# Leaving out the semaphore waits that an engine's earlier wait already covers, in a two-layer transformer kernel on 8 cores

## The chip, the cores and the metric

The kernel runs on the 8 cores of one Trainium2 chip. Every core runs the same program on its own rows. The metric is the device time in microseconds of the slowest core. Five engines of a core take part: TensorE (PE), VectorE (DVE), ScalarE (ACT), GpSimd (POOL) and SyncE (SP). Each works through its own list of instructions in order, and they meet only at semaphores.

## The reference, cut to what matters

Four sub-layers follow each other, each with a residual and a layer norm around it:

```python
x = _layernorm(x + _L0_attn_ref(x, ...))   # 16 heads, one shared K and V of width 64, softmax over 4096 keys
x = _layernorm(x + _L0_ffn_ref(x, ...))    # 4096-wide FFN, top-1 LoRA expert of 8
x = _layernorm(x + _L1_attn_ref(x, ...))   # third-order attention on a window of the last 32 keys
x = _layernorm(x + _L1_ffn_ref(x, ...))    # 8 SwiGLU experts, top-4 weights
```

The input is 4 x 4096 x 1024 in float32.

## The kernel before

Two cores share one of the 4 sequences. A core owns 2048 rows (16 tiles of 128, in the SBUF buffer `resid`) and also reads the other half for the keys and values of the first attention. The work is written as phases, one after the other:

- **kv** (`phA_kv_all`): for 32 row tiles in turn a layer norm (`ln_tile`: DVE, two tiny ACT functions at L126 and L128, DVE again), 8 transposes on PE (L523), a copy on ACT (L531), the K product (L544) and the V product (L552), and two copies on ACT (L561, L564). The ACT functions of the next tile stand behind these copies in ACT's list.
- **four rounds of q, attention, wo** (`phA_q`, `phA_attn`, `phA_wo`), each for 512 rows. Attention goes over 16 heads, and for each head over 16 key blocks kp of 256 keys. `emit_qk` (L731) makes two 512-column products into one of two PSUM slots, `emit_exp` (L742) is one exponential of 128x1024 on ACT into one of three SBUF slots, and `emit_pv` (L753) makes two products with V. PE's list has QK(kp+1) before PV(kp). The end of head h is written out after kp = 1 of head h+1 (`epilogue`): a reciprocal of 1x512 on DVE (L766), a broadcast product on PE (L770), a copy on ACT (L776) and a product on DVE (L780). It stands ahead of QK(3) in PE's list.
- **B** (`phaseB`): the first FFN, 32 groups of 9 products (L989, L995) with a ReLU on ACT (L1004) and then the second matrix (L1036), for four groups of 512 rows; the routing work (`emit_prep`, `rank_counts`) stands in between.
- **C** (`phaseC`): the windowed attention of the last 128 rows, head by head, and 16 tiles of layer norms.
- **D** (`phaseD`): routing of 16 tiles (L1337, L1357), then 8 experts x 2 halves: 32 pairs of gate and up products (L1457, L1464), each with two ACT and three DVE instructions (L1476 to L1498), and then the down product (L1517) of 8 tiles. **Out** writes the result.

`run_phase` calls a phase's function once for each engine, each time with a new object of the class `Em`. `Em` counts every semaphore (TT, VV, SS, GG are bumped by PE, DVE, ACT and POOL; the lanes LX, LW and SO by DMAs) and puts out only the instructions of its own engine. A wait is asked for by `E.w(engine, semaphore, value)` or, for a DMA, by `E.wt(engine, token)`; `E.dma` asks for one on its lane itself. Before the change each of these calls puts one wait instruction of its own into the engine's list, ahead of the instruction that it guards. So an instruction can have several waits ahead of it. The one for the exponential, in `emit_exp`:

```python
        E.w("s", "TT", qkv)           # QK(kp) is done
        E.w("s", "TT", lps[pslot])    # the PV that last read this slot is done
```

Semaphores only count up, and both waits are on TT. PE's list has PV(kp-3) before QK(kp), so the value of the second is never above that of the first.

Of the kernel before, what the change touches and what calls it, by code (L numbers as in the profile page):

```python
# [34 lines left out]
class Ctr:  # L35
    __slots__ = ("sem", "n", "step")

    def __init__(self, sem, step=1):
        self.sem, self.n, self.step = sem, 0, step
# [7 lines left out]
class Em:  # L47
    def __init__(self, k, eng, C):
        self.k, self.e, self.C = k, eng, C

    def dma(self, pool, key, f):
        idx = self.C["_pool_" + pool]
        names = LANES[pool]
        name = names[idx.n % len(names)]
        idx.n += 1
        c = self.C[name]
        self.w(key, name, c.n)
        c.n += 16
        tok = (name, c.n)
        if self.k == key:  # L60
            f(self.e).then_inc(c.sem, 16)
        return tok

    def wt(self, key, tok):
        if tok and self.k == key:
            self.e.wait_ge(self.C[tok[0]].sem, tok[1])

    def op(self, key, f, inc=None):
# [10 lines left out]

    def w(self, key, cname, val):  # L80
        if self.k == key and val and val > 0:
            self.e.wait_ge(self.C[cname].sem, val)

    def t(self, f, inc=None):
# [1482 lines left out]
def host_prep(inputs):  # L1567
# [7 lines left out]
    def ktile(w):  # L1575
        K, N = w.shape
        return np.ascontiguousarray(
            w.reshape(K // 128, 128, N).transpose(1, 0, 2).reshape(128, -1))
# [74 lines left out]
```

## Time and profile before

| | us |
|---|---|
| median of the two timed runs | 7444.8 |
| the two runs | 7669.35 and 7220.25 |
| the profiled execution, its device time | 7291.01 |
| its span, slowest core (core 3) | 7289.2 |
| spans of the eight cores | 7185.3 to 7289.2 |
| granted TensorE clock, mean over the cores of die 0 / die 1 (medians) | 0.862 / 0.872 |

A busy share is a mean over phases with different limits. The page's slices and the table by stretch show where PE is full and where the engines take turns. "Idle before" is the time for which an engine had nothing running ahead of an instruction, with what ended it. Wait instructions themselves are not shown as busy: their time is part of these idle times.

### The profile page before, as it was taken

How to read it: one execution, taken by the hardware profiler on the slowest of the kernel's cores; microseconds unless marked ns; L12 is line 12 of the kernel's file. 1: busy time of each engine (PE TensorE's matmuls, PEld its weight loads, DVE VectorE, ACT ScalarE, POOL GpSimd, SP SyncE). 2: the span in 40 equal slices, each digit the busy share in tenths (PEclk: the TensorE clock that was granted, in tenths of full speed). 3: DMA queues.
4: the chain of work that ended last, by engine and by line, in shares of the span. 5: the costliest groups of instructions: out<-in, count | busy, mean ns of one | idle time of the engine just before them, and what ended most of it. 6: DMA issues, size and time to landing. Idle time of an engine off the chain costs nothing.

```text
span 7289.2 us, 67922 instructions; the slowest of 8 cores (7185.3 to 7289.2 us)
## 1 busy us (share of the span) xinstructions
PE 5151.0 (71%) x22235; PEld 2083.4 (29%) x22235; DVE 2548.8 (35%) x5344; ACT 2241.3 (31%) x3440; POOL 246.8 (3%) x428
## 2 busy tenths in 40 slices
PE   2367577577576675673110498989989898989996
PEld 1222222222222222221000243434434343434332
DVE  6521311312213101102447543444434444444334
ACT  1257377376584110111220222222222222222211
POOL 0000000000000000000000000000000000000000
PEclk9989799799798887786555599999999999999787
DMA  2100000100100555565000223232332324232321
GB/s 65 41 12 1 12 12 1 23 1 1 24 1 14 104 93 93 105 115 92 0 0 0 41 49 64 47 66 45 56 58 47 70 47 70 47 70 47 63 36 58
DMA packets 61633, 326.06 MB, mean 45 GB/s; under 512 B 7218, under 2 KB 7490, under 8 KB 46544
## 3 DMA queue, kind: packets, MB, share of 16 engines
q0 software_dynamic: 54400, 296.50, 23.1%
q1 hardware_dynamic: 6896, 25.23, 1.0%
q8 instruction: 193, 3.16, 0.2%
q14 instruction: 144, 1.18, 0.1%
HBM read 609.63 MB, written 8.39 MB: 85 GB/s over the span
## 4 chain that ended last, share of the span: by engine, by line
PE 56%; DVE 16%; ACT 12%; DMA 7%; issue 6%; POOL 1%; DVEq 0%; ACTq 0%; POOLq 0%; SPq 0%
PE pB L1517 13%; PE pA L1457 12%; ACT pTs L742 7%; PE pA L1464 6%; PE pB L1464 6%; PE pA L753 4%; DMA wobuf<-woT 3%; DVE rrec L766 3%; PE pB L731 3%; PE pB L1036 3%; DMA wgu<-guT 2%; PE pA L989 2%; DMA wibuf<-wiT 1%; DVE lnt L143 1%; PE pB L614 1%
## 5 line engine op out<-in xcount | busy, mean ns | idle before, releaser
L742 ACT ACTIVATE pTs<-pB,cbias 128x1024 bf16<-128x1024 f32 x1024 | 1095.6, 1110 | 280.7 <-PE pB L731 275.5
L1457 PE MATMUL pA<-x3T,wgu 128*128 128x512 bf16 x4096 | 1005.8, 390 | 122.8 <-DMA wgu<-guT 104.4
L1476 ACT ACTIVATE r7D<-pA,g7mb 128x512 f32<-128x512 f32 x512 | 351.8, 687 | 2278.7 <-PE pA L1464 1696.9
L1517 PE MATMUL pB<-dnTsb,actT 128*128 128x512 bf16 x4096 | 971.7, 399 | 72.1 <-DVE actT L1498 72.1
L753 PE MATMUL pA<-pTs,vones 128*128 128x512 bf16 x2048 | 611.2, 379 | 287.2 <-ACT pTs L742 284.0
L1486 DVE SCALAR_TENSOR_TENSOR t1D<-r7D,sgD 128x512 f32<-128x512 f32 x512 | 354.4, 692 | 805.2 <-ACT sgD L1481 805.2
L766 DVE RECIPROCAL rrec<-pA 1x512 f32<-1x512 f32 x64 | 214.7, 3355 | 1128.6 <-PE pA L753 1094.9
L731 PE MATMUL pB<-qhT,kT 128*128 128x512 bf16 x2048 | 604.1, 382 | 0.5 <-ACT cbias L714 0.5
L1517 PEld LDWEIGHTS pB<-dnTsb,actT 128*128 128x128 bf16 x4096 | 405.6, 102 | 630.5 <-issue 271.7
L1457 PEld LDWEIGHTS pA<-x3T,wgu 128*128 128x128 bf16 x4096 | 381.4, 99 | 681.2 <-issue 355.1
L1464 PE MATMUL pA<-x3T,wgu 128*128 128x512 bf16 x2048 | 500.8, 389 | 0.0
L1464 PE MATMUL pB<-x3T,wgu 128*128 128x512 bf16 x2048 | 496.1, 386 | 0.0
L1532 DVE SCALAR_TENSOR_TENSOR resid<-pB,ncomb,resid 128x1024 f32<-128x1024 f32 x128 | 164.3, 1284 | 884.3 <-PE pB L1525 884.3
L1036 PE MATMUL pB<-wobuf,interT 128*128 128x512 bf16 x1024 | 285.8, 447 | 163.9 <-DMA wobuf<-woT 151.5
L1498 DVE SCALAR_TENSOR_TENSOR actT<-r7D,t1D 128x512 bf16<-128x512 f32 x512 | 354.4, 692 | 54.5 <-DVE r7D L1491 1.4
L753 PEld LDWEIGHTS pA<-pTs,vones 128*128 128x128 bf16 x2048 | 136.4, 96 | 743.6 <-issue 729.3
L1481 ACT ACTIVATE sgD<-r7D 128x512 f32<-128x512 f32 x512 | 322.3, 630 | 47.9 <-ACT r7D L1476 1.5
L126 ACT ACTIVATE stat<-stat 128x1 f32<-128x1 f32 x144 | 29.6, 206 | 911.2 <-DVE stat L124 911.1
L1059 DVE TENSOR_TENSOR ytmpB<-pB,resid 128x1024 f32<-128x1024 f32 x16 | 19.5, 1221 | 740.5 <-PE pB L1050 740.5
L1464 PEld LDWEIGHTS pA<-x3T,wgu 128*128 128x128 bf16 x2048 | 205.0, 100 | 256.9 <-issue 49.9
L989 PE MATMUL pA<-x1T,wibuf 128*128 128x512 bf16 x1024 | 252.2, 391 | 32.7 <-ACT interT L1004 18.1
L1464 PEld LDWEIGHTS pB<-x3T,wgu 128*128 128x128 bf16 x2048 | 203.2, 99 | 250.8 <-issue 39.4
(235 smaller groups left out, 3759.4 us busy)
## 6 DMA issues: line engine op xcount, KB each, us to landing
wgu<-guT POOLq DMA_DIRECT2D x256, 512.0 KB, 5.1
wobuf<-woT POOLq DMA_DIRECT2D x64, 1024.0 KB, 10.0
wibuf<-wiT POOLq DMA_DIRECT2D x32, 1024.0 KB, 8.9
dnTsb<-dnT POOLq DMA_DIRECT2D x8, 4096.0 KB, 25.9
w<-w POOLq DMA_DIRECT2D x5, 2048.0 KB, 16.5
resid<-xb SPq DMA_DIRECT2D x4, 2048.0 KB
wbuf<-wq POOLq DMA_DIRECT2D x4, 2048.0 KB, 16.2
xst<-xb SPq DMA_DIRECT2D x16, 512.0 KB
```

Of the source, the lines that this page charges most:

```text
L731: r = E.t(lambda e, kc=kc, sub=sub, slot=slot, qoff=qoff: e.matmul(pB[slot][:, sub * 512:(sub + 1) * 512], A["kT"][:, kc * 128:(kc + 1) * ...
L742: les[slot] = E.s(lambda e, slot=slot, pslot=pslot: e.activation(out=A["pTs"][:, pslot * 1024:(pslot + 1) * 1024], in_=pB[slot][:, 0:1024] ...
L753: r = E.t(lambda e, kc=kc, sub=sub, pslot=pslot, pva=pva: e.matmul(pva[:, 0:512], A["vones"][:, kc * 128:kc * 128 + 128], A["pTs"][:, pslo ...
L766: vr = E.v(lambda e, pva=pva: e.reciprocal(A["rrec"][64:65, 0:512], pva[64:65, 0:512]), "VV")
L989: E.t(lambda e, c8=c8, p=p, gid=gid, pg=pg: e.matmul(pg[:, 0:512], Bd["wibuf"][:, (gid % 2) * 4096 + c8 * 512 + (p % 4) * 128: (gid % 2) * ...
L1036: r = E.t(lambda e, p=p, pp=pp, tl=tl, tli=tli, half=half, wid=wid: e.matmul(pB[tli][:, half * 512:(half + 1) * 512], Bd["interT"][:, p * ...
L1457: E.t(lambda e, c8=c8, gid=gid, pg_ap=pg_ap, xoff=xoff: e.matmul(pg_ap, Dd["wgu"][gid % 2][:, c8 * 128:(c8 + 1) * 128], Dd["x3T"][:, c8 * ...
L1464: r = E.t(lambda e, c8=c8, gid=gid, pu_ap=pu_ap, xoff=xoff: e.matmul(pu_ap, Dd["wgu"][gid % 2][:, 1024 + c8 * 128:1024 + (c8 + 1) * 128], ...
L1476: sr7 = E.s(lambda e, so=so, pg_ap=pg_ap, j=j: e.activation(out=Dd["r7"][:, so:so + 512], in_=pg_ap, func=AF.Relu, scale=-1.0, bias=Dd["g7 ...
L1486: vt1 = E.v(lambda e, so=so: e.scalar_tensor_tensor(out=Dd["t1"][:, so:so + 512], in0=Dd["r7"][:, so:so + 512], scalar=7.0, in1=Dd["sg"][: ...
L1498: act_vv[par] = E.v(lambda e, so=so, aoff=aoff: e.scalar_tensor_tensor(out=Dd["actT"][:, aoff:aoff + 512], in0=Dd["r7"][:, so:so + 512], s ...
L1517: E.t(lambda e, kc=kc, half=half, t8=t8, pw=pw: e.matmul(pw[:, half * 512:(half + 1) * 512], Dd["actT"][:, kc * 1024 + (t8 // 4) * 512 + ( ...
```

## The change

`Em` gets a table of the highest value that its engine has waited for on each semaphore in this phase. A wait whose value is not above that is not put out. Nothing else is changed: no instruction that computes, no DMA, no order, no buffer. As the table is new with each `Em`, it starts empty in each phase.

```diff
 class Em:
     def __init__(self, k, eng, C):
         self.k, self.e, self.C = k, eng, C
+        self.hwm = {}
@@
     def wt(self, key, tok):
         if tok and self.k == key:
+            if tok[1] <= self.hwm.get(tok[0], 0):
+                return
+            self.hwm[tok[0]] = tok[1]
             self.e.wait_ge(self.C[tok[0]].sem, tok[1])
@@
     def w(self, key, cname, val):
         if self.k == key and val and val > 0:
+            if val <= self.hwm.get(cname, 0):
+                return
+            self.hwm[cname] = val
             self.e.wait_ge(self.C[cname].sem, val)
```

## Rows read from the trace of the kernel before

**Rows 1.** The page: busy time by engine, and the chain by engine

```profile
PE 5151.0 (71%) x22235; PEld 2083.4 (29%) x22235; DVE 2548.8 (35%) x5344; ACT 2241.3 (31%) x3440; POOL 246.8 (3%) x428
...
PE 56%; DVE 16%; ACT 12%; DMA 7%; issue 6%; POOL 1%; DVEq 0%; ACTq 0%; POOLq 0%; SPq 0%
```

**Rows 2.** Busy time by stretch (PE, PEld, DVE, ACT, POOL; PEclk): attention, two experts

```profile
932.00:1286.00 354.00, 275.20 (x1050) 84.62 (x1050) 61.20 (x31) 281.87 (x273) 0.00 (x0) 1.00 0.04 7
...
5315.00:5694.00 379.00, 352.65 (x1572) 148.93 (x1573) 158.58 (x212) 84.71 (x129) 17.96 (x34) 0.96 0.32 56
...
6834.00:7208.00 374.00, 364.96 (x1373) 146.69 (x1372) 140.54 (x187) 75.11 (x115) 14.25 (x27) 0.81 0.23 38
```

**Rows 3.** Timeline of attention: start, duration, engine, line; in brackets idle before

```profile
1500.94 2.12 ACT L742 ACTIVATE pTs<-pB,cbias 128x1024 bf16<-128x1024 f32 x2 [0.32 <-PE pB L731]
...
1502.17 0.13 PEld L753 LDWEIGHTS pA<-pTs,vones 128*128 128x128 bf16 x2 [0.87 <-issue]
1502.20 0.59 PE L753 MATMUL pA<-pTs,vones 128*128 128x512 bf16 x2 [0.41 <-ACT pTs L742]
...
1502.63 0.59 PE L731 MATMUL pB<-qhT,kT 128*128 128x512 bf16 x2
...
1503.38 2.12 ACT L742 ACTIVATE pTs<-pB,cbias 128x1024 bf16<-128x1024 f32 x2 [0.32 <-PE pB L731]
```

**Rows 4.** Timeline of attention from one head to the next

```profile
523.61 2.12 ACT L742 ACTIVATE pTs<-pB,cbias 128x1024 bf16<-128x1024 f32 x2 [0.92 <-PE pB L731]
...
540.51 3.35 DVE L766 RECIPROCAL rrec<-pA 1x512 f32<-1x512 f32 x1 [16.74 <-PE pA L753]
...
544.09 0.19 PEld L770 LDWEIGHTS pA<-rrec,ones 1*64 1x64 f32 x2 [0.81 <-issue]
544.12 1.04 PE L770 MATMUL pA<-rrec,ones 1*64 1x512 f32 x2 [0.34 <-DVE rrec L766]
...
545.85 1.11 ACT L742 ACTIVATE pTs<-pB,cbias 128x1024 bf16<-128x1024 f32 x1 [0.92 <-PE pB L731]
```

**Rows 5.** Timeline of kv: one row tile, and the same product of the next

```profile
201.09 0.61 PE L552 MATMUL pA<-wkv_sb,xnT 128*128 128x64 bf16 x8
...
201.78 0.21 ACT L564 CAST vones<-pA 128x64 bf16<-128x64 f32 x1 [0.28 <-PE pA L552]
...
206.22 1.01 PE L523 MATMUL pF<-idb,xnb 128*128 128x128 bf16 x8 [4.53 <-DVE xnb L145]
...
207.38 1.01 ACT L531 COPY xnT<-pF 128x1024 bf16<-128x1024 bf16 x1 [4.99 <-PE pF L523]
...
208.61 0.82 PEld L544 LDWEIGHTS pA<-xnT,wkv_sb 128*64 128x64 bf16 x8 [1.65 <-issue]
...
214.75 1.01 PE L523 MATMUL pF<-idb,xnb 128*128 128x128 bf16 x8 [4.54 <-DVE xnb L145]
```

**Rows 6.** Timeline of C: a layer norm's first instruction behind two waits

```profile
3861.35 0.69 DVE L118 BATCH_NORM_STATS2 stat<-Pf 128x6 f32<-128x512 f32 x1 [0.17 <-DVE Pf L1311]
```

**Rows 7.** Timeline of D: a pair's end, the next pair, and the down product's start

```profile
5001.97 1.89 PE L1464 MATMUL pA<-x3T,wgu 128*128 128x512 bf16 x8
...
5003.70 1.89 PE L1457 MATMUL pA<-x3T,wgu 128*128 128x512 bf16 x8
...
5024.89 0.69 DVE L1498 SCALAR_TENSOR_TENSOR actT<-r7D,t1D 128x512 bf16<-128x512 f32 x1
5026.02 1.00 PEld L1517 LDWEIGHTS pB<-dnTsb,actT 128*128 128x128 bf16 x6 [4.94 <-issue]
```

**Rows 8.** Chain in order of time: ends of the weight wait before three experts

```profile
5276.40 21.75 DMA wgu<-guT
...
5655.28 20.90 DMA wgu<-guT
...
6800.73 17.08 DMA wgu<-guT
```

**Rows 9.** One line of D, its last down tile: first and last start

```profile
L1532 DVE SCALAR_TENSOR_TENSOR resid<-pB,ncomb,resid x128: 1283/1284/1286, 4281.1 to 7229.4; 128x1024 f32<-128x1024 f32 x128
```

## The prediction

> **What bounds the kernel now.** I read the page first: no engine is full over the span, PE is busy 71%, and the chain that ended last is PE for 56%, DVE for 16% and ACT for 12% [rows 1]. Then the busy time by stretch, which splits the kernel in two kinds [rows 2]. In an expert of D, PE is busy 352.65 of 379 us: one engine streams. In an attention round ACT is busy 281.87 and PE 275.20 of 354 us: neither is full, they take turns. In kv DVE, PE and ACT take turns too, as the timeline shows: PE has stood idle 4.53 us before L523, ACT 4.99 us before L531 [rows 5]. Removed waits can matter only where engines take turns, since there every step from one engine to the next stands in the time. Then I read the timeline at such handovers, and that is where the reader should look: at the time between the end of one engine's work and the start of the next one's.
>
> Attention [rows 3]: the two exponentials that start at 1500.94 are followed by the next two at 1503.38, 2.44 us later, of which ACT is busy 2.12. The first ends at 1500.94 + 1.11 = 1502.05. PV's weight load starts at 1502.17, PV at 1502.20, QK at 1502.63, it ends at 1503.22, and the next exponential starts at 1503.38. So exp(kp), PV(kp), QK(kp+2), exp(kp+2) is a closed loop, and it sets the pace, not ACT (2.12) and not PE (8 products of 0.215 us, 1.72).
>
> **The change part by part.** It only removes wait instructions. I counted them from the code, engine by engine and phase by phase: 3161 of 14108 waits go, 1788 on PE, 1159 on ACT, 169 on DVE, 37 on POOL and 8 on SP. Of PE's 1096 and ACT's 1081 are in the four attention rounds, and 394 of PE's are in D.
>
> *Price of one wait.* The trace gives handovers with one wait and with more.
> - ACT after PE. One wait: L552 ends at 201.09 + 0.61 = 201.70 and L564 starts at 201.78, 0.08. Two: L523 ends at 207.23 and L531 starts at 207.38, 0.15 [rows 5]. The exponential with its two waits: 0.16 [rows 3]. The rows are rounded to 0.01, so a second wait costs 0.05 to 0.07; I take 0.06.
> - PE after ACT. One wait: 1502.05 to 1502.17, 0.12 [rows 3]. Two: L531 ends at 208.39 and L544's load starts at 208.61, 0.22 [rows 5]. After DVE with two: 540.51 + 3.35 = 543.86 to 544.09, 0.23 [rows 4]. With four: 5024.89 + 0.69 = 5025.58 to 5026.02, 0.44 [rows 7]. So 0.10 to 0.11 for each further wait; I take 0.11.
> - DVE: L118 behind two waits starts 0.17 after the end of the instruction that it waits for [rows 6]. No row shown has the same instruction behind one wait; the bounds are nothing and the 0.11 of PE, and I take 0.07, nearest to ACT.
>
> The Trainium skill, Advanced Engine Details and Errata, section Miscellaneous Facts, puts reading a semaphore from the sequencer at 50 to 100 ns, and the two prices above agree with it. VectorE: DVE Perf Modes, section The DRAIN you can't avoid, says that a semaphore after each of 8 copies cost nothing extra on DVE. By that rule the DVE term below would be nothing in place of 2.2 us.
>
> *Where a wait is hidden.* A wait that was satisfied long ago costs nothing if PE still has products queued. In each step of attention one of the waits that go stands between PV and QK, yet QK starts 1502.63 - 1502.20 = 0.43 us after PV, two products of 0.215 [rows 3]. In D two or three waits stand before each new pair; the pair at 5003.70 starts 1.73 us after the eight products that started at 5001.97, 0.216 each [rows 7]. So the 1033 removed waits before QK and the 302 before pairs in D are worth nothing: running products cover them. If that cover were gone, each would cost 0.11. A removed wait also gains nothing if it stands ahead of the wait that really blocks.
>
> *The sum, from handovers that are on the chain and where a removed wait follows the blocking one.*
> - Attention. One head's chain runs exp 3, 5, ..., 15, then PV, the reciprocal, L770, QK(3), and exp 3 of the next head (523.61 to 545.85) [rows 4]. On it are 7 exponentials with a second wait, and L770 with one: 7 x 0.06 + 0.11 = 0.53 us. The exponentials in between are in the same kind of loop and get shorter by the same, so they don't take over. L770 sits waiting for the reciprocal (0.34 idle), so that leg stays the longer one. Of the 64 heads I count 60, since at each round's start the clock is low and PE is the limit. 60 x 0.53 = 31.8.
> - kv. The next tile's norm waits in ACT's list behind this tile's last copy, so each tile is one chain of 214.75 - 206.22 = 8.53 us [rows 5]. L523, L544 (PE) and L531 (ACT) each lose a second wait: 31 x (0.11 + 0.11 + 0.06) = 8.7.
> - q. 16 tiles of the same form, with two waits on PE (L614, L645) and two on ACT (L601, L625): 16 x 0.34 = 5.4.
> - D. Before L1517 three waits behind the blocking one, 15 times: 15 x 0.33 = 5.0. Routing, L1357, 15 x 0.11 = 1.7.
> - B. Before L1036 about 15 waits: 1.7. Its other removed waits stand first or are covered.
> - wo and C. L118 32 times on DVE at 0.07, 2.2; ACT's L1211 15 times at 0.06, 0.9. Together 3.1.
> - POOL and SP: 45 waits ahead of DMA issues that are made early. Nothing; if each was on the path at PE's price, 5.
>
> Sum 57.4 us. Against the profiled execution: 7291.0 - 57.4 = 7234 us. The two runs shown lie at 7220.25 and 7669.35, so their median of 7444.8 is a mean of two unlike numbers. The profiled execution lies near the faster, and the forecast is for an execution of its kind. From 7220.25 the same sum gives 7163.
>
> **The rivals.**
> - *Nothing is gained.* Something next to the shortened loop takes over, or the handover ends on the slower of two legs anyway. For it: DVE's reciprocal (3.35) and the exponentials (1.11) stay as they are. Against: ACT stands idle 0.32 of each 2.44 and PE has idle time too [rows 3], and in kv nothing that matters runs beside the chain. Time 7291.
> - *Every removed wait counts,* since the engine's instruction stream is the limit. Then 1788 x 0.11 + 1159 x 0.06 + 169 x 0.07 = 197 + 70 + 12 = 279, and the time is 7012, faster by 3.8%. Against it speaks the spacing of 0.215 across a wait in rows 3 and 7. It passes 2% (146 us) when 89 us beyond my sum, about 810 of PE's waits, prove exposed.
> - *Slower: a lower granted clock for longer.* From 6834 on the granted clock is 0.81 of the 2.4 GHz level, where the expert before it in rows 2 has 0.96. The full-clock expert runs from 5276.40 + 21.75 = 5298.15 to 5655.28, 357.1 us; the last one from 6817.81 to 7229.4, 411.6 us [rows 8, 9]. So an expert at 0.81 costs 54 us more. The change makes PE denser in attention (0.53 us of each head) and lets D begin earlier; if the lower clock came three experts sooner, the gain is gone twice over: 7234 + 163 = 7397. Slower by 2% (7437) needs 3.7 experts more; all of the other 6.8 give 7601, which is near the slower run shown. For it: such a run exists already. Against: that run was of the kernel before, and the whole attention round at full clock (1.00) [rows 2] with PE at 78% did not bring it on.
>
> **How the numbers follow.** The forecast has 0.78, nothing gained 0.06, every wait 0.06, the clock 0.10, of which 0.07 is beyond 2% and 0.03 within. About 2% is what a measurement of this kernel can tell from no change. So faster 0.06, same 0.78 + 0.06 + 0.03 = 0.87, slower 0.07. The forecast alone spans 7150 to 7270: from 7291 the prices at their low ends and only attention and kv counted give 7291 - (60 x 0.45 + 31 x 0.25) = 7256, and from 7220.25 with a third more waits exposed it is 7144. The range is 7140 to 7400: down to that, and up to three experts more at the lower clock.
>
> **What would show it.** In the profile after: the page's instruction count falls from 67922 by 3161. Pairs of exponentials start 2.38 us apart and not 2.44, and ACT's idle before L742 falls from 0.32 to 0.26. The kv tiles come 8.25 us apart and not 8.53. L770's load starts 0.12 after the reciprocal, L1517's 0.12 after L1498. A full-clock expert still takes 357 us. I am wrong if the pairs of exponentials keep their distance, if experts at the same clock get shorter or longer, or if the lower clock covers another part of D than before.

## The result, and the profile after

| | before | after |
|---|---|---|
| median of all timings, us | 7635.29 (10) | 7472.83 (11) |
| lowest timings, us | 7219.94, 7220.25, 7223.72, 7226.57 | 7157.43, 7157.84, 7158.30 |
| profiled execution, us | 7291.01 | 7157.53 |
| ratio after to before | | 0.991, 95% interval 0.9891 to 0.993 |

In the other timings of both kernels (7601 to 7729 before, 7304 to 7683 after) the granted clock of one die, in 7585.86 of both, is lower than in the lowest ones, whatever the kernel, so the ratio comes from the lowest ones alone. The change takes 0.9% off, clear of nothing but below 2%. That is 64 us, where the sum of the prediction was 57.4. The forecast of 7234 and its range of 7140 to 7400 missed the median of all timings, 7472.83; the three lowest timings lie inside the range.

The page of the changed kernel: instructions, busy time, granted clock in 40 slices, and the chain.

```profile
span 7156.0 us, 64761 instructions; the slowest of 8 cores (7119.6 to 7156.0 us)
...
PE 5065.1 (71%) x22235; PEld 2058.0 (29%) x22235; DVE 2548.6 (36%) x5344; ACT 2239.5 (31%) x3440; POOL 246.9 (3%) x428
...
PEclk9989799799898887786555599999999999999998
...
PE 56%; DVE 17%; ACT 12%; DMA 8%; issue 5%; POOL 1%; DVEq 0%; ACTq 0%; POOLq 0%; SPq 0%
```

The count has fallen from 67922 to 64761, by exactly the 3161 waits that were counted. DVE's and ACT's busy time is as in [rows 1]. PE's is 86 us less, but the count of products is the same: core 3 of the profile before ran part of D at the lower clock [rows 2], and this one did not. So the difference of the two profiled spans, 133 us, is not the change's. I compare a core whose granted clock over D is 0.97 in both, which is called full clock below.

One attention pair in the timeline of the changed kernel (L749 is L742 before, L760 is L753, L738 is L731), to be held against [rows 3]:

```profile
1471.08 2.12 ACT L749 ACTIVATE pTs<-pB,cbias 128x1024 bf16<-128x1024 f32 x2 [0.26 <-PE pB L738]
...
1472.30 0.13 PEld L760 LDWEIGHTS pA<-pTs,vones 128*128 128x128 bf16 x2 [0.81 <-issue]
1472.33 0.59 PE L760 MATMUL pA<-pTs,vones 128*128 128x512 bf16 x2 [0.35 <-ACT pTs L749]
...
1472.76 0.59 PE L738 MATMUL pB<-qhT,kT 128*128 128x512 bf16 x2
...
1473.45 2.12 ACT L749 ACTIVATE pTs<-pB,cbias 128x1024 bf16<-128x1024 f32 x2 [0.26 <-PE pB L738]
```

The exponential ends at 1472.19 and PV's load starts at 1472.30, 0.11 later (before 0.12). QK ends at 1473.35 and the exponential starts at 1473.45, 0.10 later, where it was 0.16. All of the gain of this loop is in that one handover, and the pairs are 2.37 apart where they were 2.44.

The end of a head (L773 is L766, L777 is L770), against [rows 4], and a tile of kv (L530 is L523, L538 is L531, L551 is L544), against [rows 5]:

```profile
529.12 3.35 DVE L773 RECIPROCAL rrec<-pA 1x512 f32<-1x512 f32 x1 [16.08 <-PE pA L760]
...
532.59 0.19 PEld L777 LDWEIGHTS pA<-rrec,ones 1*64 1x64 f32 x2 [0.76 <-issue]
```

```profile
202.00 1.01 PE L530 MATMUL pF<-idb,xnb 128*128 128x128 bf16 x8 [4.42 <-DVE xnb L152]
...
203.10 1.01 ACT L538 COPY xnT<-pF 128x1024 bf16<-128x1024 bf16 x1 [4.83 <-PE pF L530]
...
204.23 0.82 PEld L551 LDWEIGHTS pA<-xnT,wkv_sb 128*64 128x64 bf16 x8 [1.48 <-issue]
...
210.26 1.01 PE L530 MATMUL pF<-idb,xnb 128*128 128x128 bf16 x8 [4.42 <-DVE xnb L152]
```

The load behind the reciprocal starts 532.59 - 532.47 = 0.12 after it (before 0.23). In kv the copy starts 0.09 after the transposes (before 0.15), the product's load 0.12 after the copy (before 0.22), and a tile takes 8.26 us (before 8.53).

The down product's start in D (L1524 is L1517, L1505 is L1498), against [rows 7], and the norm's first instruction in C (L125 is L118), against [rows 6]:

```profile
4973.52 0.69 DVE L1505 SCALAR_TENSOR_TENSOR actT<-r7D,t1D 128x512 bf16<-128x512 f32 x1
4974.32 0.13 PEld L1524 LDWEIGHTS pB<-dnTsb,actT 128*128 128x128 bf16 x2 [4.62 <-issue]
```

```profile
3791.09 1.22 DVE L1318 TENSOR_TENSOR Pf<-attC,resid 128x1024 f32<-128x1024 f32 x1
3792.41 0.69 DVE L125 BATCH_NORM_STATS2 stat<-Pf 128x6 f32<-128x512 f32 x1
```

The load starts 4974.32 - 4974.21 = 0.11 after its input, where it was 0.44 with three more waits. The norm starts 3792.41 - 3792.31 = 0.10 after its input, where it was 0.17 with one more wait. That is the price of 0.07 on DVE, which the prediction had to take between two bounds.

Where the kernel's stages end, on core 4 of both profiles, from the first and last start of the exponentials and of the down product's last step in the views by line. Before:

```profile
L742 ACT ACTIVATE pTs<-pB,cbias x1024: 1105/1113/1115, 430.2 to 2272.4; 128x1024 bf16<-128x1024 f32 x171
L1532 DVE SCALAR_TENSOR_TENSOR resid<-pB,ncomb,resid x128: 1283/1284/1286, 4284.7 to 7154.3; 128x1024 f32<-128x1024 f32 x128
```

After:

```profile
L749 ACT ACTIVATE pTs<-pB,cbias x1024: 1105/1113/1115, 421.9 to 2217.7; 128x1024 bf16<-128x1024 f32 x171
L1539 DVE SCALAR_TENSOR_TENSOR resid<-pB,ncomb,resid x128: 1283/1284/1286, 4230.7 to 7096.4; 128x1024 f32<-128x1024 f32 x128
```

| stretch, us | before | after | gain | sum of the prediction |
|---|---|---|---|---|
| start to the first exponential (kv, first q) | 430.2 | 421.9 | 8.3 | 8.7 + 1.4 |
| first to last exponential: four rounds | 1399.9 | 1366.9 | 33.1 | 31.8 |
| and the three gaps between them (wo, q) | 442.3 | 428.9 | 13.3 | 5.6 |
| to the first down product (last wo, B, C, routing) | 2012.3 | 2013.1 | -0.8 | about 5 |
| to the last down product (D) | 2869.6 | 2865.7 | 3.9 | 5.0 |
| end | 59.8 | 59.6 | 0.3 | 0 |

The fourth line is not still. On the eight cores of one profile it takes 1999 to 2019 us before and 1997 to 2013 after, and 1993 to 2015 in the experiments that leave B and C as before. One execution of the changed kernel with two waits more in attention (below) has it at 1983 to 2000, and its time of 7137.67 is 20 us below the changed kernel's. So a gain of 5 us can't be seen there. The part of it in C can: from the first to the last norm start of its 16 tiles all eight cores take 1.1 us less, 15 times 0.07.

The fifth line isn't still either. Over the cores at full clock D takes 2855 to 2872 us before and 2848 to 2866 after. That core 4 gained 3.9 there does not confirm the 5.0; the handover of 0.44 that became 0.11 does. An expert, from its first down tile to that of the next, takes 371 to 382 us before and 371 to 380 after at full clock, so experts at the same clock kept their length, as the prediction asked.

The total of core 4, 58.1 us, is near the sum of 57.4 partly by luck. The other three cores of its die, at full clock in both profiles, gained 53, 71 and 73 us.

### The profile page after: what moved, and what is told of

Its sections match the earlier page's. It is cut to its first block, busy times and chain, and to the rows that moved or that the text cites. A ratio compares the mean times of both kernels' runs of the same rounds, so it can differ in the third digit from the quotient of the medians.

```text
span 7156.0 us, 64761 instructions; the slowest of 8 cores (7119.6 to 7156.0 us)
## 1 busy us (share of the span) xinstructions
PE 5065.1 (71%) x22235; PEld 2058.0 (29%) x22235; DVE 2548.6 (36%) x5344; ACT 2239.5 (31%) x3440; POOL 246.9 (3%) x428
## 4 chain that ended last, share of the span: by engine, by line
PE 56%; DVE 17%; ACT 12%; DMA 8%; issue 5%; POOL 1%; DVEq 0%; ACTq 0%; POOLq 0%; SPq 0%
PE pB L1524 13%; PE pA L1464 12%; ACT pTs L749 7%; PE pA L1471 6%; PE pB L1471 6%; PE pA L760 4%; DMA wobuf<-woT 3%; PE pB L738 3%; DVE rrec L773 3%; PE pB L1043 3%; DMA wgu<-guT 2%; PE pA L996 2%; DMA wibuf<-wiT 1%; DVE lnt L150 1%; PE pB L621 1%
## 5 line engine op out<-in xcount | busy, mean ns | idle before, releaser
L749 ACT ACTIVATE pTs<-pB,cbias 128x1024 bf16<-128x1024 f32 x1024 | 1093.7, 1111 | 249.8 <-PE pB L738 247.4
L1464 PE MATMUL pA<-x3T,wgu 128*128 128x512 bf16 x4096 | 980.0, 382 | 127.8 <-DMA wgu<-guT 107.6
L1524 PE MATMUL pB<-dnTsb,actT 128*128 128x512 bf16 x4096 | 938.5, 389 | 67.6 <-DVE actT L1505 67.6
L760 PE MATMUL pA<-pTs,vones 128*128 128x512 bf16 x2048 | 610.3, 379 | 262.3 <-ACT pTs L749 260.5
L773 DVE RECIPROCAL rrec<-pA 1x512 f32<-1x512 f32 x64 | 214.7, 3355 | 1098.7 <-PE pA L760 1098.7
L738 PE MATMUL pB<-qhT,kT 128*128 128x512 bf16 x2048 | 602.6, 381 | 0.5 <-ACT cbias L721 0.5
L1524 PEld LDWEIGHTS pB<-dnTsb,actT 128*128 128x128 bf16 x4096 | 398.1, 100 | 600.5 <-issue 166.1
L1471 PE MATMUL pA<-x3T,wgu 128*128 128x512 bf16 x2048 | 487.8, 382 | 0.0
L1505 DVE SCALAR_TENSOR_TENSOR actT<-r7D,t1D 128x512 bf16<-128x512 f32 x512 | 354.5, 692 | 54.5 <-DVE r7D L1498 1.4
L760 PEld LDWEIGHTS pA<-pTs,vones 128*128 128x128 bf16 x2048 | 136.1, 96 | 718.1 <-issue 703.6
L738 PEld LDWEIGHTS pB<-qhT,kT 128*128 128x128 bf16 x2048 | 192.8, 97 | 281.4 <-issue 54.4
## 6 DMA issues: line engine op xcount, KB each, us to landing
wobuf<-woT POOLq DMA_DIRECT2D x64, 1024.0 KB, 10.1
```

The costliest lines, as they stand in the source:

```text
L738: r = E.t(lambda e, kc=kc, sub=sub, slot=slot, qoff=qoff: e.matmul(pB[slot][:, sub * 512:(sub + 1) * 512], A["kT"][:, kc * 128:(kc + 1) * ...
L749: les[slot] = E.s(lambda e, slot=slot, pslot=pslot: e.activation(out=A["pTs"][:, pslot * 1024:(pslot + 1) * 1024], in_=pB[slot][:, 0:1024] ...
L760: r = E.t(lambda e, kc=kc, sub=sub, pslot=pslot, pva=pva: e.matmul(pva[:, 0:512], A["vones"][:, kc * 128:kc * 128 + 128], A["pTs"][:, pslo ...
L773: vr = E.v(lambda e, pva=pva: e.reciprocal(A["rrec"][64:65, 0:512], pva[64:65, 0:512]), "VV")
L1464: E.t(lambda e, c8=c8, gid=gid, pg_ap=pg_ap, xoff=xoff: e.matmul(pg_ap, Dd["wgu"][gid % 2][:, c8 * 128:(c8 + 1) * 128], Dd["x3T"][:, c8 * ...
L1471: r = E.t(lambda e, c8=c8, gid=gid, pu_ap=pu_ap, xoff=xoff: e.matmul(pu_ap, Dd["wgu"][gid % 2][:, 1024 + c8 * 128:1024 + (c8 + 1) * 128], ...
```

## The experiments

Each kernel below is the changed one but for its edit (three of them put the covered waits out again outside the place that is named), and the numbers are of cores at full clock in the stretch that is read. An attention round is the time from its first to its last exponential. The kernels that test one wait or one stage have one or three timings each (7137.67 to 7708.11 us), from which nothing is concluded; their rows are read.

**Attention only.** Covered waits are left out in attention and put out everywhere else.

```diff
             if val <= self.hwm.get(cname, 0):
-                return
+                if not self.cut:
+                    self.e.wait_ge(self.C[cname].sem, val)
+                return
@@ def phA_attn
+    E.cut = True
```

> Covered waits are left out in the four attention rounds only; everywhere else they are all put out, as before. Theory (a wait that was behind the blocking one costs about 0.06 us on ACT and 0.11 on PE in each handover): pairs of exponentials start 2.38 us apart and not 2.43, each attention round lasts 342 us from its first to its last exponential (kernel before 350, changed kernel 342), the kv tiles stay 8.53 apart. Rival (the gain in attention came from somewhere else, such as the shorter instruction list): a round lies clearly above 342.

Core 4, two pairs of exponentials, and two copies of kv (L755 is L742 before, L543 is L531):

```profile
1501.62 2.12 ACT L755 ACTIVATE pTs<-pB,cbias 128x1024 bf16<-128x1024 f32 x2 [0.26 <-PE pB L744]
...
1504.00 2.12 ACT L755 ACTIVATE pTs<-pB,cbias 128x1024 bf16<-128x1024 f32 x2 [0.26 <-PE pB L744]
```

```profile
207.37 1.01 ACT L543 COPY xnT<-pF 128x1024 bf16<-128x1024 bf16 x1 [4.99 <-PE pF L535]
...
215.90 1.01 ACT L543 COPY xnT<-pF 128x1024 bf16<-128x1024 bf16 x1 [4.99 <-PE pF L535]
```

Rounds of 341.9, 341.3, 342.6 and 341.7 us, pairs 2.38 apart, kv tiles at 8.53 as before. The gain of a stage comes from the waits of that stage, and the length of the rest of the instruction list has no part in it.

**Only the waits that were called hidden.** 1324 of PE's waits are left out, those ahead of QK and of the pairs in D, and all others put out.

```diff
+        E.cut = True
         E.w("t", "SS", les[slot])
+        E.cut = False
```

> Only the 1324 waits that I called hidden are left out: those ahead of QK in attention (1022) and ahead of the gate and up pairs in D (302). All others are as before. Theory: running products cover them, so nothing moves: rounds of 350 us, pairs of exponentials 2.43 apart, a full-clock expert of 375 to 379. Rival (every wait costs PE's 0.11): 1022 x 0.11 / 4 = 28 us less in each round, and 4 us less in an expert.

Core 1:

```profile
1525.00 2.12 ACT L756 ACTIVATE pTs<-pB,cbias 128x1024 bf16<-128x1024 f32 x2 [0.32 <-PE pB L745]
...
1527.43 2.12 ACT L756 ACTIVATE pTs<-pB,cbias 128x1024 bf16<-128x1024 f32 x2 [0.32 <-PE pB L745]
```

Pairs 2.43 apart with the old 0.32 of idle time, and rounds of 349.9, 350.1, 349.6 and 349.6: not even 1 us where the rival wanted 28. In D the rival wanted 33 us; the six cores at full clock take 2849 to 2866 us, before 2855 to 2872, so it is refuted there too, but less sharply, since cores differ by as much. Three quarters of PE's removed waits are worth nothing that these numbers can show.

**Two and eight more waits under the cover.** The same place from the other side: satisfied waits are added ahead of QK.

```diff
         E.w("t", "SS", les[slot])
+        if les[slot]:
+            E.again("t", "SS", les[slot], 2)      # 8 in the second kernel
```

> The changed kernel with two more satisfied waits on PE ahead of each QK of attention. Theory: PV's two products run for 0.43 us, and 2 waits take 0.21, so they stay covered: a round of 342 us, pairs 2.38 apart. Rival (each wait costs): a pair has one QK on its chain, so 0.21 more: pairs 2.59 apart and a round of about 342 + 16 x 6.5 x 0.21 = 364.

> The changed kernel with eight more satisfied waits on PE ahead of each QK of attention. Theory: the cover is 0.43 us and holds about 4 waits; the other 4 cost 0.11 each, so a step gets 0.44 longer: pairs 2.82 apart, a round about 342 + 16 x 6.5 x 0.44 = 388. Rival (no cover, each wait costs): 0.85 longer, pairs 3.2 apart. Rival (satisfied waits cost nothing): 2.38.

Core 4 with two more, and then core 4 with eight more:

```profile
539.22 2.12 ACT L756 ACTIVATE pTs<-pB,cbias 128x1024 bf16<-128x1024 f32 x2 [0.26 <-PE pB L745]
...
541.60 2.12 ACT L756 ACTIVATE pTs<-pB,cbias 128x1024 bf16<-128x1024 f32 x2 [0.26 <-PE pB L745]
```

```profile
540.02 2.17 ACT L756 ACTIVATE pTs<-pB,cbias 128x1024 bf16<-128x1024 f32 x2 [0.68 <-PE pB L745]
...
542.84 1.11 ACT L756 ACTIVATE pTs<-pB,cbias 128x1024 bf16<-128x1024 f32 x1 [0.64 <-PE pB L745]
```

With two more: 2.38 apart, and the fourth round is 341.9, that of the changed kernel is 341.8. With eight more: 2.85 apart in the median and rounds of 394 to 396 us. Eight waits at 0.105 to 0.11 take 0.84 to 0.88 us and cost 0.47, so 0.37 to 0.41 us of them, between three and four waits, lie under PV's two products. The expectation had 2.82 and 388.

**Two more waits behind the blocking one on ACT.**

```diff
         E.w("s", "TT", lps[pslot])
+        E.again("s", "TT", qkv, 2)
```

> The changed kernel with two more satisfied waits on ACT behind the one that blocks, ahead of each exponential. Theory (0.055 to 0.06 us for each, since ACT has nothing queued that would cover them): pairs of exponentials 2.49 to 2.50 apart and not 2.38, an attention round of 342 + 16 x 7 x 0.11 = 354 us. Rival (the second wait of the kernel before was dear only by where it stood): under 2.45.

Core 0, first round:

```profile
525.62 2.12 ACT L755 ACTIVATE pTs<-pB,cbias 128x1024 bf16<-128x1024 f32 x2 [0.37 <-PE pB L743]
...
528.11 2.12 ACT L755 ACTIVATE pTs<-pB,cbias 128x1024 bf16<-128x1024 f32 x2 [0.37 <-PE pB L743]
```

2.49 apart, idle 0.37 where the changed kernel has 0.26, a first round of 354.8 us. Each wait behind the blocking one costs 0.055 us on ACT. On cores 2 to 7 all four rounds ran at full clock, and took 354.2 to 354.8 us. On cores 0 and 1 the granted clock was 0.85 to 0.90 in the later rounds, and they took 366 to 373.

**The q and wo phases only.**

```diff
 def phA_q(E, sh, A, st, qq):
+    E.cut = True
 def phA_wo(E, sh, A, st, qq):
+    E.cut = True
```

> Covered waits are left out in the q and wo phases only (65 on PE, 33 on ACT, 41 on DVE). From a round's last exponential to the next round's first one the kernel before takes 152 to 153, 144 and 145 us, the changed kernel 149.4, 139.5 and 140.0, 13 us less in the three together, where my prices give 1.9 each, 5.6 together. The kernel with only attention changed also moved them, by -1.9, -1.2 and +0.8. Theory A (the prices are right, and the rest is that the granted clock changes at other places of q and wo when the work ahead of them ends earlier): about 1.9 less each, give or take 1.5. Theory B (I missed waits that stand in the way in these phases): the whole 13 us. Attention stays at 350, kv tiles at 8.53.

On core 4 the three gaps took 149.0, 141.3 and 141.4 us, 10.5 less than before in total; on core 3 149.8, 140.3 and 139.1, 12.3 less. Core 4 has the smallest gain: the eight cores take 428 to 432 us in total, and before, the six at full clock in attention 441 to 442. Attention stayed at 350 and kv tiles at 8.53. With only attention changed the total is 439 to 440 on the cores at full clock. So the gain of the gaps is made by the waits of q and wo, as theory B has it.

But it is not made of handovers alone. Core 4, from a tile's first q product (L614) to its transposes (L645), with the length behind the window and the granted clock third from the end: the third and the fourth tile of the second gap before, and the fourth after (L621 and L652):

```profile
1396.40:1402.96 6.56, 4.95 (x17) 1.80 (x18) 0.00 (x0) 1.02 (x1) 0.00 (x0) 0.79 0.01 1
1414.08:1421.73 7.65, 6.33 (x16) 2.12 (x17) 0.00 (x0) 1.02 (x1) 0.00 (x0) 0.64 0.00 0
```

```profile
1382.72:1389.00 6.28, 5.01 (x16) 1.80 (x17) 0.00 (x0) 1.02 (x1) 0.00 (x0) 0.77 0.00 0
```

The same work with the same waits takes 6.56 us in one tile and 7.65 in the next, where more of its products ran at 1.2 GHz. Before, five of the twelve tiles of the three gaps take 7.5 us or more, after, one does. An estimate from the starts of the tiles on core 4: what each takes above the shortest of its kernel adds up to 11.8 us before and 4.6 after. So about 7 of the 13.3 us are the granted clock's, which changes between 1.2 and 2.4 GHz at other places of the tiles once the waits are gone, and about 6 are the handovers', near the 5.6 of the sum. Theory A had this mechanism and wrongly held that q's and wo's own waits would bring only 1.9 a gap with it.

**The stalest wait first.** An engine's waits are kept back until its next instruction, and the one that lies furthest back is put out first.

```diff
+        todo = sorted(((behind(n, v), i, n, v) for n, (v, i) in last.items()),
+                      key=lambda r: (r[0], r[1]), reverse=True)
+        for _, _, n, v in todo:
+            self.e.wait_ge(self.C[n].sem, v)
```

> The changed kernel, in which an engine's waits are kept back until its next instruction and the one that lies furthest back is put out first, so that the one that blocks comes last. Theory (a wait behind the blocking one costs, one ahead of it doesn't): gains where two waits that are both needed stand in the wrong order: the reciprocal of attention (16 times a round, 0.07, so 341 in place of 342), ACT's first instruction of a pair in D (0.06 each, where PE waits for DVE), and C. In all 5 to 15 us below the changed kernel, so 0.989 to 0.990 of the kernel before. Rival (order does not matter): 0.991. Of the ten to eleven timings of either kernel so far more than half were in the upper group (7.30 to 7.73 ms); I expect that of this kernel too, whatever its waits.

Its lowest two timings are 7152.93 and 7160.05, those of the kernel before beside it 7211.78 to 7221.03; the ratio of 0.9958 has an interval of 0.9886 to 1.0031. On core 0 the rounds are 342.2, 341.8, 341.3 and 342.2 and the down products take 2865.8, as in the changed kernel. Inconclusive by time, and no stage shows the gain that I expected of it.

**The last wait carried by the instruction.** ACT's and DVE's instructions carry the last of their waits, PE's and the DMA issues' too in two further kernels, and DVE's alone in a fourth.

```diff
+        ride = todo.pop() if todo and ride_ok else None
@@ op
+            ride = self.flush(self.k in RIDE)     # RIDE = ("s", "v")
             ins = f(self.e)
+            if ride:
+                ins._wait_ge(self.C[ride[2]].sem, ride[3])
```

> As the kernel with the stalest wait first, and the last wait of an ACT or DVE instruction is carried by the instruction itself and not by a wait instruction of its own (6185 fewer wait instructions). Theory (a wait instruction costs its engine's price, 0.055 on ACT and 0.07 on DVE, wherever it is exposed, the last one too): pairs of exponentials 2.32 apart and not 2.38, kv tiles 8.26 less four ACT and five DVE handovers, 0.57, so 7.7; attention 4 x 6.2, kv 18, C and routing some 30 us less, together 70 us below the changed kernel, 0.98 of the kernel before. Rival (the engine checks a carried wait as slowly as an instruction of its own): nothing moves against the kernel with the stalest first.

> As the one before, and PE's last wait is carried by the product too. Theory: another 0.11 in each handover to PE: pairs of exponentials 2.21 apart, kv tiles 7.5, and 0.967 to 0.975 of the kernel before. Rival (on PE a carried wait costs as much): 0.98 and 2.32.

> As the kernel in which ACT's and DVE's last wait rides on the instruction, but DVE's only. That one took 0.96 of the kernel before where I expected 0.98. Theory (the surplus is DVE's: long runs of small dependent DVE instructions in the routing of B and D and in C, each with a wait of its own): the stretch from the last exponential to the first down tile, 1985 to 2013 us in the kernels without carried waits and 1890 with them, is under 1930 here, while pairs of exponentials stay 2.38 apart. Rival (the surplus is ACT's): this stretch stays above 1960. kv tiles: five DVE handovers at 0.05 to 0.07 less than 8.26, so 7.95 to 8.0.

> The last wait of every instruction, DMA issues too, is carried by the instruction, with the stalest first among the others: 2498 wait instructions are left with PE's, ACT's and DVE's carried, 2038 here. Theory: as the kernel with PE's carried too, 6845 to 6855 us for its lower group of timings, since SP and POOL issue early: 0.948 to 0.952 of the kernel before. Rival (POOL's waits hold the weight loads of B): 10 to 20 us less still. The upper group of timings appears here too.

| carried on | ratio to before, 95% | pair | kv tile | to the first down product |
|---|---|---|---|---|
| nothing (changed kernel) | 0.991, 0.9891 to 0.993 | 2.38 | 8.26 | 1997 to 2013 |
| DVE | one timing, 7065.59 | 2.38 | 8.05 | 1912 to 1928 |
| ACT, DVE | 0.9596, 0.9568 to 0.9624 | 2.32 | 7.87 | 1886 to 1903 |
| ACT, DVE, PE | 0.9564, 0.9418 to 0.9709 | 2.24 | 7.75 | 1876 to 1888 |
| all, DMA issues too | 0.9415, 0.929 to 0.954 | 2.24 | 7.75 | 1862 to 1878 |

The intervals of the last two rows are wide: 6942.25 of the kernel with PE's carried went into one, and 7240.00 to 7312.56 of the kernel before into the other. By the lowest timing of each the two ratios are 0.950 and 0.948.

Attention with ACT's and DVE's carried (core 5), and with all (core 2):

```profile
1519.32 2.12 ACT L773 ACTIVATE pTs<-pB,cbias 128x1024 bf16<-128x1024 f32 x2 [0.20 <-PE pB L762]
...
1521.63 1.11 ACT L773 ACTIVATE pTs<-pB,cbias 128x1024 bf16<-128x1024 f32 x1 [0.20 <-PE pB L762]
```

```profile
1521.96 0.61 PE L787 MATMUL pA<-pTs,vones 128*128 128x512 bf16 x2 [0.20 <-ACT pTs L776]
...
1524.20 0.61 PE L787 MATMUL pA<-pTs,vones 128*128 128x512 bf16 x2 [0.20 <-ACT pTs L776]
```

The idle time before the exponential goes 0.32, 0.26, 0.20: one wait less each time. With ACT's and DVE's carried the pair of 2.32 came as expected. The whole did not: the lowest timing is 6915.86, about 240 us below the changed kernel, where I expected 70. Of that, 34 us are the four rounds (25 expected), 22 the time to the first exponential (18 for kv), and 27 the gaps. The last column fell by about 110 us, where I expected some 30 for C and routing, and D by about 40, which I had not counted at all. DVE's waits alone make 85 of the 110, so theory DVE holds for that column, and its rival is refuted. Over the whole, cores at full clock take 6992 to 7020 us with DVE's carried, about 130 below the changed kernel: DVE's share is about half, and ACT's the other.

PE's carried waits brought less than I expected: pairs 2.24 apart and not 2.21, kv tiles 7.75 and not 7.5. A load of PE starts 0.05 us after its input where it was 0.11, 0.06 less and not 0.11. The rival (2.32) is refuted all the same. DVE's kv tile came to 8.05, just above the 7.95 to 8.0.

Routing's inner loop in B shows DVE's part, before and with DVE's waits carried (L206 is L177, L213 is L184):

```profile
2557.93 0.17 DVE L177 TENSOR_TENSOR sAB<-lgtB 128x5 f32<-128x5 f32 x1
...
2558.61 0.16 DVE L177 TENSOR_TENSOR sAB<-lgtB 128x4 f32<-128x4 f32 x1
```

```profile
2450.20 0.17 DVE L206 TENSOR_TENSOR sAB<-lgtB 128x7 f32<-128x7 f32 x1
...
2450.75 0.17 DVE L206 TENSOR_TENSOR sAB<-lgtB 128x6 f32<-128x6 f32 x1
```

A turn takes 0.68 us with two wait instructions and 0.55 with two carried waits, so each costs 0.07 there, and 224 turns of B and D make 30 us; the rest of the 85 is not divided. The three lowest timings of the kernel with all carried are 6839.60, 6840.06 and 6842.97; the lowest two of the kernel before beside them are 7216.00 and 7219.21, which makes 0.948, as expected. It beats the kernel before and the changed one. What the DMA issues add to it is not shown: the lowest timing is 14 us below that of the kernel without them, the rival wanted 10 to 20, and cores and executions of one kernel scatter by as much.

## Why the prediction was right or wrong

**The step that failed is the third rival's chance, and with it the time.** I took the profiled execution as the kind of execution that is forecast, and gave a lower granted clock in D 0.10, although one of the two timings shown, 7669.35, lay 449 us up and its price (54 us an expert, 371 for 6.8 experts) already led to it. In the 11 timings after, eight lie between 7304 and 7683; I had written 7601 for the lower clock through all of D, and two timings lie at 7602.48 and 7603.02 and one above them at 7682.69. The median of all, 7472.83, lies above my range, by the clock and not by a wait. One profile of the experiment with the hidden waits holds both cases in one execution. Core 1 and core 7 from 4300 to 7100 us, with PE's busy time and products first and the granted clock third from the end:

```profile
4300.00:7100.00 2800.00, 2621.17 (x11703) 1106.89 (x11702) 1182.40 (x1579) 632.02 (x960) 133.03 (x252) 0.97 0.31 56
```

```profile
4300.00:7100.00 2800.00, 2660.95 (x10704) 1087.98 (x10703) 1086.84 (x1454) 582.63 (x884) 124.08 (x235) 0.87 0.29 52
```

In the same time the core at 0.87 has made 10704 products and the one at 0.97 11703. The clock, not a wait, sets those timings. D takes 3106 us on core 7 and 2866 on core 1, 240 us more for the same instructions.

My argument against this rival read only core 3: its attention round at full clock. In the same profile of the kernel before, cores 0 and 1 had a granted clock of 0.81 through their first round, and took 373 us where the others took 350. So the lower clock isn't bound to D, and a round costs 23 us more at it. And the sign that I had named, the lower clock covering another part of D than before, did come: in the profile after no core has it there. The part of the rival that said the change would bring it on has no support: six of the 10 timings before and eight of the 11 after are of this kind, too few to tell the kernels apart. What does bring it on was not tried and stays open.

**The price of one wait** was right: 0.06 on ACT (measured 0.055), 0.11 on PE (from 0.23 to 0.12 at L777, from 0.22 to 0.12 ahead of kv's product, from 0.44 to 0.11 for three in D: 0.10 to 0.11), 0.07 on DVE (from 0.17 to 0.10 at L125). The 0.10 to 0.11 of PE lies at the upper end of the 50 to 100 ns that the prediction quotes and just above it, so "agree" was a little too much for that price. The DVE term was not nothing, as the quoted rule of the 8 copies would have it.

**What is hidden** was right, and the runs show it from both sides: 1324 waits left out moved nothing, two more cost nothing, and of eight more between three and four were covered.

**The sum**, 57.4, is near the 64 of the lowest timings, but one term was mis-sized. Attention is 31.8 against 33.1, kv with the first q 10.1 against 8.3. q and wo came to 13.3 in three gaps where I had 5.6, and the surplus is, by the estimate above, mostly the granted clock's, which changes at other places of the tiles and which the sum left out. D's 5.0 is shown by its handovers, not by its length, and B and routing can't be told from nothing, since that stretch moves by over 10 us from core to core. So three terms carry the agreement, one too small by 8 us, and the total hides it.

**Nothing gained** and **every wait counts** are refuted, the first by attention's 33 us, the second by the experiment with the hidden waits.

**Against 7291.0.** Core 3 of that profile had the lower clock for the last experts [rows 2, 8, 9], and takes 2948 us in D where core 4 takes 2870. The base at full clock was 7220.25, one of the two timings shown. From there the sum gives 7163, as the text said, and the three lowest timings are 7157 to 7158. I should have made that number the forecast for full clock and spread the chance over both kinds.

## What to carry to other kernels

A wait instruction costs its engine's time only where the engine is already waiting: look at the gap between one engine's end and the next one's start, count the wait instructions behind the blocking one, and leave alone those under running products. Waits already covered by an earlier one are worth removing in stages where engines take turns, but the wait instruction that is needed costs about as much again, and letting the instruction carry it brought about four (ACT and DVE) to five times as much (all) here. When the timings of a kernel fall into two groups, a forecast of the median needs a chance for each group first and a sum of nanoseconds second.

## What the runs showed of the hardware

- A further wait instruction behind the one that blocks cost 0.055 us on ACT, 0.10 to 0.11 on PE and 0.07 on DVE. Carried by the instruction, the blocking wait itself cost 0.06 less a handover on ACT and 0.07 less on DVE, but on PE only 0.06 less, a little more than half.
- While two 512-column products ran (0.43 us), PE took between three and four satisfied waits without a gap.
- The granted clock was 0.81 of 2.4 GHz over a whole stretch of 374 us, between its two levels of 2.4 and 1.2 GHz [rows 2]. It isn't a mean of the two: inside that stretch, from 6946 to 7150 us, PE was busy all the time and the granted clock was 0.81 too.
- The lower level came to pairs of a die's cores at different times: in the profile before, cores 0 and 1 had 0.81 through the first attention round and 0.97 in D, cores 2 and 3 the full clock in that round and 0.94 over D.
- The Trainium skill, VectorE: DVE Perf Modes, section The DRAIN you can't avoid, says that a semaphore after each of 8 copies cost nothing extra. It does not say whether an instruction of its own waited for it. Here such an instruction was not free on DVE: 0.07 us for each, in the loop of 0.68 us above as well as behind the instruction of 1.22 us ahead of L125.
